# First layer's attention: normalisation and scaling by GpSimd, roots in slots without additions, and scores ahead of maxima in each slot on the matrix engine

## What is computed

```python
q = (xn @ w_q).reshape(b, n, HEADS, DIM_HEAD).transpose(0, 2, 1, 3)
k, v = jnp.split(xn @ w_kv, 2, axis=-1)        # then heads, null keys and values in front
q = _l2norm(q) * q_scale                       # t / max(norm(t), 1e-12)
k = _l2norm(k) * k_scale
sim = jnp.einsum('bhid,bhjd->bhij', q, k) * ATTN_SCALE + dist * slopes
sim = jnp.where(causal_mask[None, None], neg, sim)
out = jnp.einsum('bhij,bhjd->bhid', jax.nn.softmax(sim, axis=-1), v)
return out.transpose(0, 2, 1, 3).reshape(b, n, HEADS * DIM_HEAD) @ w_out
```

## Time and profile before

| what | us |
|---|---|
| median of three runs | 2028.43 |
| the profiled execution, its own time | 2043.86 |
| its span, first to last instruction | 2042.1 |
| TensorE busy over the span | 1633.4 (80%) |
| VectorE busy | 1223.0 (60%) |
| ScalarE busy | 886.8 (43%) |
| GpSimd busy | 764.7 (37%) |
| the first layer's attention, eight pairs | 312 to about 1290 |

### The profile page before, as it was taken

The page is one execution under the profiler, slowest core; times in us unless marked ns, Lnnn a source line. Parts: engine busy times, 40 slices in busy tenths (PEclk is TensorE's granted clock), DMA queues, the critical chain, the costliest instruction groups (busy, mean ns, idle before and its releaser), DMA issues. The chain is left out here.

```text
span 2042.1 us, 35995 instructions
## 1 busy us (share of the span) xinstructions
PE 1633.4 (80%) x13931; PEld 819.6 (40%) x13931; DVE 1223.0 (60%) x2150; ACT 886.8 (43%) x1438; POOL 764.7 (37%) x423
## 2 busy tenths in 40 slices
PE   2468459879889898898989998345998889888887
PEld 2246325435354353544535443224654323333232
DVE  5323357686766757576576661481266877777761
ACT  0112215536456463564635455012322655555566
POOL 1500553564656656465564768260000111400000
PEclk9879759989899998999989999567998977888888
DMA  4113210000000000000000000123320000000000
GB/s 156 52 32 107 48 24 12 7 12 22 7 19 11 18 17 7 24 12 12 17 7 20 12 12 12 65 79 94 93 74 27 13 13 28 9 18 2 2 7 17
DMA packets 57109, 62.00 MB, mean 30 GB/s; under 512 B 12890, under 2 KB 42862, under 8 KB 56046
## 3 DMA queue, kind: packets, MB, share of 16 engines
q1 hardware_dynamic: 52846, 51.32, 8.1%
q0 software_dynamic: 4096, 8.40, 1.6%
HBM read 40.34 MB, written 18.48 MB: 29 GB/s over the span
## 5 line engine op out<-in xcount | busy, mean ns | idle before, releaser
L1582 POOL TENSOR_TENSOR a_prob_sum<-a_prob_sum,a_prob 128x1024 f32<-128x1024 f32 (+2 forms) x224 | 499.9, 2232 | 239.1 <-ACT a_prob L1530 218.2
L1530 ACT ACTIVATE a_prob<-a_st,a_table 128x512 f32<-128x512 f32 (+3 forms) x640 | 352.7, 626 | 358.3 <-PE a_st L1408 219.5
L1628 DVE TENSOR_REDUCE a_maxima<-a_ring 128x16 f32<-128x512 f32 (+3 forms) x640 | 352.8, 600 | 127.2 <-PE a_ring L1340 102.5
L1914 DVE TENSOR_REDUCE a_maxima<-a_mx 128x1 f32<-128x512 f32 (+3 forms) x640 | 352.3, 605 | 122.1 <-PE a_mx L1898 59.7
L2158 ACT ACTIVATE a_prob<-a_st 128x1024 f32<-128x1024 f32 (+3 forms) x320 | 269.0, 894 | 183.3 <-PE a_st L2076 102.4
L1435 PE MATMUL a_ot<-a_prob,a_values 128*64 128x512 f32 (+3 forms) x1280 | 289.0, 570 | 0.0
L1340 PE MATMUL a_ring<-a_k_hi,a_q_hi 64*128 64x512 f16 (+3 forms) x640 | 166.1, 373 | 94.2 <-DVE a_maxima L1628 71.6
L1898 PE MATMUL a_mx<-a_ks,a_qs 32*128 32x512 f16 (+3 forms) x640 | 188.3, 393 | 39.9 <-DVE a_maxima L1914 36.7
L2092 PE MATMUL a_ot<-a_prob,values_all 128*32 128x512 f32 (+3 forms) x1280 | 179.8, 638 | 0.2 <-ACT a_sums L2150 0.2
L2041 POOL DMA_INDIRECT a_back<-expert_out,slot_from x32 | 30.3, 948 | 347.7 <-ACT a_prob L2158 347.7
L1898 PEld LDWEIGHTS a_mx<-a_ks,a_qs 32*128 32x128 f16 x640 | 46.4, 93 | 246.8 <-DVE a_maxima L1914 173.8
(11 more groups left out here) (260 smaller groups left out, 2600.2 us busy)
## 6 DMA issues: line engine op xcount, KB each, us to landing
a_rden<-rden_wide SPq DMA_DIRECT2D x64, 128.0 KB, 2.9
f_w<-in_w SPq DMA_DIRECT2D x28, 256.0 KB, 2.8
expert_in<-zeros SPq DMA_DIRECT2D x5, 1024.0 KB, 11.2
f_rows<-expert_in SPq DMA_DIRECT2D x16, 256.0 KB, 3.7
expert_out<-f_result SPq DMA_DIRECT2D x16, 256.0 KB, 2.2
shared_w<-in_w SPq DMA_DIRECT2D x12, 256.0 KB, 3.1
a_table<-in_head_table SPq DMA_DIRECT2D x16, 140.5 KB, 2.2
parts<-part_t SPq DMA_DIRECT2D x4, 512.0 KB
```

Of the source, the lines that this page charges most:

```text
L1530: e = act.activation(prob[:, s % NPROB, a, c0:QW], ps_st[s % 2][:, a, c0:QW], ACT.Exp, bias=table[x][:, a, at:at + 1])
L1582: pool.tensor_tensor(into[:, :, c0:QW], into[:, :, c0:QW], here[:, :, c0:QW], ALU.add).then_inc(added, 2 if r == TPQ - 2 else 1)
L1628: dve.reduce_max(maxima[:, qt // TPQ, a, qt % TPQ, at:at + count], bank[:, 0:hi - lo].rearrange("p (w k) -> p w k", k=WINDOW), AX_X).then_ ...
L1914: dve.reduce_max(own.maxima[:, qt // TPQ, a, qt % TPQ, n:n + 1], bank[:, 0:hi - lo], AX_X).then_inc(done, 1)
```

## The change

- TensorE: in each slot below the end of the pair, `scores` of that slot stands ahead of the slot's units `one`. Before, the units of the even slot stood ahead of two scores in a row.
- `scale_out` moves from VectorE to GpSimd, to behind the addition of the same slot. VectorE's `invert` now waits that the scaling before it is done.
- For pairs prepared by `NEXT0` (pairs 3 to 7) `normalise` moves to GpSimd: groups 0 and 1 at slot 39, groups 2 and 3 at slot 3 of the next pair, after that slot's addition, if any. Pairs 0, 1 and 2 are still normalised by VectorE.
- `NEXT0` begins at slot 9 instead of 11; its roots stand at slot 23 (parts 0 and 1) and slot 24 (parts 2 and 3). Part 0 waits that the normalises of the pair before are done.
- The `v` units stand at slots 2 to 6 instead of 4 to 8.

```diff
-        self.newton = {qk + 2 * NQB + 2 + k: k for k in range(NEWTON + 1)}
+        self.newton = {qk + 2 * NQB + 2 + k: (k,) for k in range(NEWTON + 1)}
-NEXT0 = Ahead0(11)
+NEXT0 = Ahead0(9)
+NEXT0.newton = {ENDS0[2]: (0, 1), ENDS0[2] + 1: (2, 3)}
+POOL_NORM0 = {ENDS0[3]: (0, 1), ENDS0[0]: (2, 3)}
-V_AT0 = {4 + u: u for u in range(V_UNITS0)}
+V_AT0 = {2 + u: u for u in range(V_UNITS0)}
@@ TensorE, step
                 for n, x, s, one, two in slots0(first, last)[0]:
+                    if x < 2:
+                        if s == 0:
+                            pe.wait_ge(null_loaded[x], 16 * i + 16)
+                        if SLOTS0[s][1] == 0:
+                            pe.wait_ge(row_loaded[SLOTS0[s][0]], 64 * i + 32 * x + 32)
+                        if n >= 2 or not first:
+                            pe.wait_ge(exp_done, begun + n - 1)
+                        scores(x, s)
                     for unit in one:
                         put(unit, base, 2 * i + unit.what[0], i)
-                    if n % 2 == 0 and x < 2:
-                        if s == 0:
-                            pe.wait_ge(null_loaded[x], 16 * i + 16)
-                        for m in (n, n + 1):
-                            if SLOTS0[m % NS0][1] == 0:
-                                pe.wait_ge(row_loaded[SLOTS0[m % NS0][0]], 64 * i + 32 * x + 32)
-                            if m >= 2 or not first:
-                                pe.wait_ge(exp_done, begun + m - 1)
-                            scores(x, m % NS0)
@@ GpSimd
+            def normalise(pair, g):
+                rows = raw[:, TPQ * g:TPQ * g + TPQ, :].rearrange("p t (g d) -> p t g d", d=DH0)
+                r = rnorm[:, 4 * TPQ * g:4 * TPQ * (g + 1)].rearrange("p (t g) -> p t g", g=4)
+                pool.wait_ge(newton_step, pair * NEWTON_STEPS + NEWTON_STEPS)
+                pool.tensor_tensor(rows, rows, r.unsqueeze(3).to_broadcast([P, TPQ, 4, DH0]), ALU.mult).then_inc(qn_done, 1)
+
+            def scale_out(qb, count):
+                pool.wait_ge(rden_loaded, 32 * count + 32)
+                pool.wait_ge(ot_read, count + 1)
+                pool.tensor_tensor(out_t[:, :], out_raw[qb % 2][:, :], rden[:, :], ALU.mult).then_inc(scaled, 1)
+
             def step(i, first=False, last=False):
-                for n in range(2 * NS0):
-                    add(i, n, n // NS0, n % NS0, first, last)
+                for n in range(2 * NS0 + (TAIL0 if last else 0)):
+                    x, s = divmod(n, NS0)
+                    if x < 2:
+                        add(i, n, x, s, first, last)
+                    if s in SCALE_AT0 and is_born(x, SCALE_AT0[s], first):
+                        scale_out(SCALE_AT0[s], i * (2 * NQB) + outs_before(x, SCALE_AT0[s]))
+                    ahead = 2 if s == ENDS0[3] else 1
+                    if x < 2 and x + ahead < (2 if last else 4) and not (first and x + ahead < 3):
+                        for g in POOL_NORM0.get(s, ()):
+                            normalise(2 * i + x + ahead, g)
@@ VectorE
                 if part == 0:
                     dve.wait_ge(ss_done, pair * NQB + NQB)
+                    if not (isinstance(pair, int) and pair == 0):
+                        dve.wait_ge(qn_done, pair * NQB)
             def invert(count):
+                if is_past(count):
+                    dve.wait_ge(scaled, count)
-                    if s in SCALE_AT0 and is_born(x, SCALE_AT0[s], first):
-                        scale_out(SCALE_AT0[s], i * (2 * NQB) + outs_before(x, SCALE_AT0[s]))
-                        if s in at.newton:
-                            inverse_roots(2 * i + pair, at.newton[s])
-                        if s in at.norm:
+                        for part in at.newton.get(s, ()):
+                            inverse_roots(2 * i + pair, part)
+                        if at is not NEXT0 and s in at.norm:
                             normalise(2 * i + pair, at.norm[s])
```

More of the change, by code:

```diff
@@ L1692, in invert @@
             def invert(count):
+                if is_past(count):
+                    dve.wait_ge(scaled, count)
                 dve.wait_ge(den_turned, 32 * count + 32)
                 dve.reciprocal(rden_rows[:, :], den_rows[:, :]).then_inc(inverted, 1)
-            def scale_out(qb, count):
-                dve.wait_ge(rden_loaded, 32 * count + 32)
-                dve.wait_ge(ot_read, count + 1)
-                dve.tensor_tensor(out_t[:, :], out_raw[qb % 2][:, :], rden[:, :], ALU.mult).then_inc(scaled, 1)
             def step(i, first=False, last=False):
```

## The result

The changed kernel took 2026.45 us (median of 20 runs, 2016.56 to 2037.90) against 2039.35 us for the kernel before, run beside it (20 runs, 2022.00 to 2052.17). The ratio is 0.9941, with a 95% interval of 0.9921 to 0.9961: a gain of 12 us, where 66 were forecast and the range began at a gain of 30. (The median of before is higher here than the 2028.43 of three runs; the ratio is of runs made side by side.) Some executions show a lower granted clock and take longer; the ratios leave them out and so need not be the quotient of the medians beside them, and of one kernel, old_order_roots_19_24, only such an execution was profiled. The profiled execution spans 2027.7 us.

A forecast was written before the change was run, and what follows sets the result against it. TensorE was taken to set the pace in the middle pairs. Gains of 11.5 us in each of five (57), 4 in pair 0, 5 in pair 6 and 0 in pair 7 made 66, from 2028.4 to 1962 us; range 1925 to 1998.

The forecast's parts named there:

- normalises and scaling, clock, GpSimd's side: Middle pairs: VectorE relieved from slot 25 on gains 4.3 us, TensorE's fuller clock 3.5, GpSimd's added work costs 1.8.
- roots, two parts in slots 23 and 24: Middle pairs: root instructions beside an idle GpSimd take 0.2 us each, the 2.24 wait at slot 23 goes; gain 2.2.
- scores ahead of the units: Middle pairs: scores between transposes and first maxima cover four waits of 0.81 to 0.86 us; gain 3.3.
- Its lower bound, 0: Roots in middle pairs: no gain if the idle GpSimd's cover is missed and 3.5 us come back at slot 23.
- Clock: TensorE in middle pairs: granted clock rises to 0.98 or more; gain 3.5 us, bounds 0 and 5.5.
- Pair 0: First pair: keeps VectorE normalises and four-slot roots, loses the scaling ahead of a wait at slot 29; gain 4 us.
- Pair 7: Last pair: GpSimd sets the pace, its added scalings offset VectorE's relief in block 1; gain 0.
- Pair 6: 3.6 us for transposes, 2.4 for the scaling's wait, 0.7 small ones, less 1.7 for the scaled output; gain 5.
- rival 1: GpSimd sets the pace from slot 25 to slot 1: each middle pair gains 3.5 us less, 1980 us; chance 0.20.
- Rival 4: Slots 1 and 3: transposes wait for GpSimd's normalise, kernel slower, some 2060 us at 12 us each; chance 0.05.
- Rival 2: Middle pairs: VectorE's waits for busy GpSimd only change name, slow clock stays; 24 us gained, 2004 us; chance 0.12.
- The rule of the Trainium skill: VectorE and GpSimd: offloading between them "might not help" because of their common read port; not used in the sum.

The follow-up runs named there:

- old_order_roots_19_24: after_old_order with one root part per slot, in slots 19, 22, 23 and 24; 2018.09 us, ratio 0.9881 to the kernel before.
- old_order_roots_21_24: after_old_order with one root part per slot, in slots 21, 22, 23 and 24; 2007.60 us, ratio 0.9819 to the kernel before.
- after_old_order: The changed kernel with TensorE's order of before (units ahead of scores again); 2011.64 us, ratio 0.9898 to the kernel before.
- best_roots_21_23: old_order_roots_21_24 with the root parts in slots 21, 22 and 23 (two in slot 23); 1996.96 us, ratio 0.9856 to the kernel before.
- order_only: The kernel before with only TensorE's new order, each slot's scores ahead of its units; 2031.12 us, ratio 0.9977 to the kernel before.
- scale_only: The kernel before with only the scaling moved to GpSimd; ratio 0.9906 to the kernel before.
- norm_only: The kernel before with only the normalises of pairs 3 to 7 moved to GpSimd; ratio 0.9884 to the kernel before.
- best_again: old_order_roots_21_24 unchanged, run again on one chip with best_roots_21_23; 2002.40 us, ratio 0.9842 to the kernel before.

## Why the prediction was wrong, point by point

The sum for a middle pair, forecast and measured. The measured terms follow one path through the kernels, from before (124.5) by old_order_roots_21_24 (117.4) and after_old_order (120.2) to the changed kernel (122.5):

```
step                                        forecast   measured
normalises and scaling, clock, GpSimd's side   +6.0      +7.1
roots, two parts in slots 23 and 24            +2.2      -2.8   (alone -1.9)
scores ahead of the units                      +3.3      -2.3   (alone +0.7)
sum                                           +11.5      +2.0
```

The first row holds three terms of the prediction (4.3, 3.5 and -1.8), which no run measured apart.

**Roots: the step that failed.** The prediction said "GpSimd is idle for 7.04 us up to 780.90" and put thirteen instructions of 0.22 into that gap. The gap was read from a trace in which the stall was still there: the addition of slot 25 waits for exponentials, and these for scores, and TensorE made them late by the wait of 2.24 at slot 23 and the slow clock behind it (0.78 from there to the addition; the earlier trace rows is behind the later wait at slot 30). That wait came from the roots, and the slow clock with it. With them gone from slots 21 and 22, the gap is 2.69 us, and the addition falls on the roots again. The trace of before had a sign of it in pair 6, which has no roots and no projection units: the gap ahead of this addition is 1.39 us there. And in best_roots_21_23, where a wait of 2.38 stands at slot 23 again, the gap is 7.04 again. First before, then best_roots_21_23:

```profile
1144.98 2.35 POOL L1578 TENSOR_TENSOR a_prob_sum<-a_prob 128x1024 f32<-128x1024 f32 x1 [1.39 <-issue]
```

```profile
762.98 2.35 POOL L1580 TENSOR_TENSOR a_prob_sum<-a_prob 128x1024 f32<-128x1024 f32 x1 [7.04 <-ACT a_prob L1532]
```

In pair 3 twelve of the thirteen did take about 0.2 and one took 1.85. Pair 3 is the mildest: in the other four middle pairs two are long, 0.93 and 2.23. This is 1.6 us more than forecast in pair 3 and 2.7 in the others, where TensorE waits 5.0 to 5.2 us at slots 24 and 25 in each. The other half is that I costed the instructions, and not what stands behind them: in slot 24 `turn` and `den` need ring banks whose maxima stand behind parts 2 and 3. The prediction named these queues for other steps and not for this one. Its lower bound, 0, was the case of a missed cover; a loss was left out without a reason. That the runs show both signs (slots 22 and 23 shorter by 3.5, slots 24 and 25 longer by 6.2) settles it.

**Scores ahead of the units.** The cover works as forecast: of four waits of 0.81 to 0.86, one of 0.3 is left. The sentence that failed is "this opens no wait unless VectorE is late". VectorE is not done in several places where two units follow each other closely (the waits of 0.37 and 0.21 in slot 10 above), and these slots pay: order_only against before, between weighted sums, 1.1 us in slots 10 and 11, 0.4 in 12 and 13, 0.2 in 36 and 37, 0.5 in 38 and 39. And in order_only more than half of the 3.3 is lost in slots 0 to 9 themselves. (Between the two units stood two scores, not "weighted sums and scores"; the 1.7 us is the same.) In the changed kernel VectorE is also late at slot 39. There the raising of the maxima lies beside GpSimd's normalises:

```profile
692.12 4.09 POOL L1590 TENSOR_TENSOR a_raw<-a_raw,a_rnorm 128x1024 f32<-128x1024 f32 x2
```

```profile
692.22 2.23 DVE L1674 TENSOR_TENSOR a_level<-a_maxima,a_table 128x400 f32<-128x400 f32 x1
```

and TensorE waits 0.95 us at slots 0 and 1 for maxima, where the version with the old order waits 0.25. Used only where the transposes are, the order is worth 1.4 us in its own slots.

**Normalises and scaling: right, a little better than forecast.** A normalise on GpSimd costs 1.98 us and not 2.5, a scaling 1.27 as forecast. The Trainium skill (GPSIMD Engine Reference, 4.1 Engine selection) puts GpSimd at about twice VectorE's time for two inputs; the rows agree for the scaling, 1.27 against 0.68 undisturbed, and have 1.98 against 1.20 for the normalise. The waits of 2.24 at slot 23 and 3.31 at slot 30 are gone; behind slot 25 the longest wait in pair 3 is 0.68. TensorE waits 0.44 us for the scaled output in middle pairs (0.7 forecast) and in pair 6 1.91 (1.7 forecast):

```profile
757.91 1.13 PE L1393 MATMUL a_ring<-a_w_out,a_out_t 128*128 128x128 f32 x8 [0.44 <-POOL a_out_t L1596]
```

```profile
1120.58 1.26 PE L1393 MATMUL a_ring<-a_w_out,a_out_t 128*128 128x128 f32 x8 [1.91 <-POOL a_out_t L1596]
```

**Clock.** 0.98 was forecast and 0.96 came: the long wait moved to slots 24 and 25, and the slow stretch with it. Over slots 20 to 25 the granted clock is 0.83 to 0.85 in the middle pairs, where it was 0.90 to 1.00.

**The rest.** Pair 0: 1.2 us for 4, from which nothing follows, since this pair takes between 135.9 and 144.9 us in the profiles of this document. Pair 7: 2.7 us where none was forecast, 111.4 to 108.7; scale_only has most of it (109.3) and norm_only none (111.9), so it comes with the scaling. Pair 6: 1.0 us longer, where 5 were forecast. The waits listed in its timeline fell from 9.8 to 6.5 us, the new 1.91 included. What the sum left out is the clock behind this new wait. Windows of 10 us from the projection's start, first before, then the changed kernel:

```profile
1131.80:1141.80 10.00, 10.00 (x150) 6.16 (x150) 5.44 (x12) 3.88 (x10) 9.43 (x5) 1.00 0.01 2
```

```profile
1120.60:1130.60 10.00, 10.00 (x127) 6.14 (x127) 2.61 (x8) 2.85 (x6) 8.65 (x4) 0.66 0.01 2
```

Slots 18 to 21 of pair 6 take 14.4 us for 10.0. The same wait of 1.9 did not always have this price: these slots take 14.7 us in best_again, and 11.9 in old_order_roots_21_24, the same kernel, whose clock stays at 1.00 there. Why is open.

**The rivals.** ScalarE never waits for GpSimd in middle pairs, and GpSimd is busy for 82.5 us of 122: rival 1 falls. Rival 4 falls too, the transposes don't wait for the normalises. Rival 2 is half right: waits changed their name, though not because of the longer GpSimd queue but through the two reorderings, which no rival had priced with a loss. The rule of the Trainium skill beside it (Perfetto Trace Analysis, Optimizing Scalar/DVE Operations), that moving work between VectorE and GpSimd might not help, is not borne out here: the moves bring 7.1 us of a pair.

## What to carry to other kernels

An idle gap of an engine that waits for the stalled one is part of the stall: before work is put into it, shift the trace as if the stall were gone, and see whether the gap is still there. Small instructions in an engine's stream are costed by the first instruction behind them that frees a buffer, not by their own time; here one part per slot, or two in slot 23 and none in slot 24, was better than two in slots 23 and 24 each. An order that covers a wait should be used in the slots that have the wait, since elsewhere it only brings units closer to the readers they depend on.

## What the runs showed of the hardware

In a chain of small VectorE instructions beside GpSimd's additions, not each one waits but every second: 2.27, 0.20, 2.34, 0.22, 2.25, 0.22 us, where alone each takes 0.2. The maxima, reductions that read the ring in PSUM, took 1.29 us for two (770.54 in the changed kernel) although the addition of 2.34 us began meanwhile. The Trainium skill (SBUF — State Buffer, Who interferes with whom) has both: the two engines share one pair of ports as an exclusive lock, which a reduction on this chip never takes, a `tensor_scalar` may take, and an instruction with two SBUF inputs needs for its second one; the rows agree with the waits and with the reductions that have none. An in-place product with a broadcast last axis (1024 columns, 1.98 us) is cheaper on GpSimd than an addition of the same width (2.34 to 2.5 us).
